# First layer, batch 0: routing logits after the projections, expert comparisons between copies, q and k scaled separately, experts in the last three steps

## The chip, the cores and the metric

The kernel runs on one core of a Trainium2 chip. The core has TensorE (PE in the profile; PEld is its weight load), VectorE (DVE), ScalarE (ACT), GpSimd (POOL) and SyncE (SP), each with its own in-order queue of instructions; semaphores order them. The metric is the device time of one execution, in microseconds (us).

## The reference, cut to what matters

Four layers run in a row over x of 8 x 512 tokens of 128 features. Layer 0, where nearly all of the change lies, is

```
xn = layernorm(x)
q, k, v = split(xn @ Wqkv)                     # 16 heads of 8
q, k = rms_norm(q, q_scale), rms_norm(k, k_scale)
attn = softmax(q k^T / sqrt(8)) v @ Wproj + bproj
logits = xn @ gate_w.T + gate_b                # 10 experts, the last 2 are empty
probs = softmax(logits); keep the top 2 of 10; renormalise over the true ones -> combine_w
ffn  = sum_e combine_w[:, e] * (xn @ expert_w[e] + expert_b[e])     # 8 true experts
x = x + attn + ffn
```

## The kernel before, in words

Layer 0 is two blocks. At the end of a block all engines meet, and only then does the next begin.

**layer0_norm** loads x and the weights and normalises x over 8 batches of 512 tokens. At its end, gate_logits (L264 to L274) multiplies each of the 32 tiles of 128 tokens by the 128x10 gate matrix, each fp32 product showing as two matmul records in the trace. When all are done, VectorE adds the gate's bias (L344), and the block ends.

**layer0_mix** is written out by hand, one queue per engine, over 8 batches of 16 steps. One step s handles 4 heads and 128 keys: TensorE computes `scores` in two halves (L708), ScalarE exponentiates each half (L494), and two steps later TensorE multiplies them with v (`times_v`, L722), four steps adding up in one bank. VectorE copies that bank out after each four (`copy_o`, L545), and the next group of four waits for that copy. Scores, projections, mean squares and the replicated q and k all go through a ring of three PSUM slots, whose order is the list ring_order0: a use waits until its slot's last user was read. So scores (0, 4) half 0 waits until `take_qk(1)` (L516) has read the projection of batch 1, which is issued in step 2.

Ahead of batch 0 come: `project` (q and k, L670), `project_v` (L677), VectorE's copies of them (L516, L522), GpSimd's squares (L462), `mean_square` (L684), ScalarE's `rms` chain of four activations over [128, 1024] (L473 to L479), `scale_qk` (L528 to L533: multiply, rounded high part, low part), `replicate` (L696) and `take_rep` (L538), which puts the copies into the stacks that scores reads. Two replicates, q and k of the first heads, stand ahead of step 0; the other two are issued in steps 0 and 1.

The routing of all tokens runs once, in batch 0: `route_start` (maximum and subtraction, L574, L576), ScalarE's exponential (L483), `route_probs` (L580 to L584), `precedence` (L303: 19 comparisons of each expert's probabilities with the others'), the rest of `route` (L590 to L605), TensorE's `turn_cw` (L755, two transposes into the bank ps_y), and VectorE's copy to cw_rows (L624). SP then stores that to DRAM and loads it back spread over all partitions (cwb, 2 MB, L452, and cwT, L453). `weigh` (L553) multiplies xn by one expert's weights, into three buffers in turn, and `expert` (L741) adds that expert's product up in ps_y. In batch 0 the experts are issued two a step in steps 12 to 15, in later batches one a step from step 8.

VectorE's queue ahead of and in batch 0 is, before: route_start, take_qk(0), take_v(0), route_probs, scale_qk(0), take_rep(0, 0), take_rep(0, 1), take_rep(0, 2), take_rep(0, 3), take_qk(1), precedence and route, wait for turn_cw, cw_rows, copy_o(0, 0), take_v(1), copy_o(0, 1), weigh 0 to 2, scale_qk(1), weigh 3, copy_o(0, 2), weigh 4 to 7, take_rep(1, 0), take_rep(1, 1). TensorE's turn_cw is issued in step 3.

## Time and profile before

| | |
|---|---|
| time, median of 3 runs (lowest to highest) | 1919.44 us (1919.16 to 1919.61) |
| the profiled execution's own time | 1919.56 us |
| its span | 1917.8 us |
| its mean granted TensorE clock | 0.95 |
| PE busy over the span | 1765.0 us (92%) |
| DVE, ACT, POOL busy | 53%, 44%, 17% |
| the mix block's batch 0 begins its scores at | 55.74 us |
| batch 1 begins its scores at | 121.24 us |
| batch 2 begins its scores at | 169.74 us |

The profile is of one execution. Its timeline lists instructions in order: start (us from the span's start), duration, engine and line, output<-inputs, shapes, count of a merged run, and in brackets the idle time before it and who ended that. A view of windows gives, for each stretch, the busy time of each engine and the granted TensorE clock, 1.00 being 2.4 GHz and 0.50 being 1.2 GHz.

### The profile page before, as it was taken

Reading aid. Unit: us, or ns where it says so; the run is one execution under the profiler, and the core shown is the slowest. Engines: PE = TensorE matmul, PEld = TensorE weight load, DVE = VectorE, ACT = ScalarE, POOL = GpSimd, SP = SyncE. Lnnn points to the kernel's source line nnn. Section 1 sums busy time; section 2 is a strip of 40 time slices with the busy share of each in tenths; the row PEclk is TensorE's granted clock in tenths of the full one; section 3 lists DMA queues with packets and bytes.
Section 4 is the critical chain, followed back from the end, with each engine's and each line's share of the span. In section 5 each row is a group of like instructions: output and inputs, shape, how many; then the busy total and the mean of one; then the engine's idle time right before and its main releaser. Section 6 shows DMA issues by size and latency. Waiting matters only on the chain. (4 is left out here: it accounts for less than half of the span.)

```text
span 1917.8 us, 23240 instructions
## 1 busy us (share of the span) xinstructions
PE 1765.0 (92%) x8678; PEld 1032.3 (54%) x8678; DVE 1014.4 (53%) x1676; ACT 845.4 (44%) x1025; POOL 329.3 (17%) x274
## 2 busy tenths in 40 slices
PE   6599999998887998999999999999999978999995
PEld 4222222222553445787878787878787824444442
DVE  3454545444675444544545454545445456777665
ACT  4467777785433333343434333333434243434341
POOL 1000000000463002112121212020303022232222
PEclk8689999998777999999999999999999989999998
DMA  1222222122002640000000000000000010000001
GB/s 72 41 51 45 45 45 45 45 45 115 1 1 71 157 126 1 1 1 1 1 2 1 1 1 1 1 1 1 1 1 1 1 52 1 0 0 0 0 0 44
DMA packets 19120, 48.95 MB, mean 26 GB/s; under 512 B 784, under 2 KB 1680, under 8 KB 18128
## 3 DMA queue, kind: packets, MB, share of 16 engines
q1 hardware_dynamic: 19024, 47.63, 10.2%
q8 instruction: 65, 1.06, 0.2%
q14 instruction: 31, 0.25, 0.0%
HBM read 45.14 MB, written 2.36 MB: 25 GB/s over the span
## 5 line engine op out<-in xcount | busy, mean ns | idle before, releaser
L494 ACT ACTIVATE probs<-ps_ring 128x1024 f32<-128x1024 f32 x256 | 246.1, 1024 | 126.6 <-PE ps_ring L708 123.9
L1765 PEld LDWEIGHTS ps_o<-v,probs 128*128 128x128 f32 x2048 | 235.3, 192 | 31.0 <-issue 25.6
L1765 PE MATMUL ps_o<-v,probs 128*128 128x129 f32 x2048 | 248.1, 278 | 1.7 <-ACT probs L1490 1.2
L1490 ACT ACTIVATE probs<-ps_ring 128x1024 f32<-128x1024 f32 x128 | 126.9, 1024 | 212.4 <-PE ps_ring L1746 212.3
L722 PE MATMUL ps_o<-probs,v 128*32 128x512 f32 x1024 | 140.1, 621 | 13.1 <-DVE o_sb L545 13.1
L1571 DVE TENSOR_REDUCE negmax<-ps_o 128x2 f32<-128x1024 f32 x64 | 78.5, 1226 | 137.2 <-PE ps_o L1721 137.2
L1958 POOL TENSOR_TENSOR rs<-r,state 128x512 f32<-128x512 f32 x64 | 81.6, 1275 | 206.3 <-DVE state L2050 202.6
L1483 ACT ACTIVATE xn<-ps_ring,pack 128x512 f32<-128x512 f32 x64 | 40.5, 685 | 162.6 <-PE ps_ring L1330 162.6
L708 PEld LDWEIGHTS ps_ring<-q_stack,k_stack 32*128 32x128 f32 x512 | 31.9, 188 | 123.2 <-issue 103.0
L1584 DVE RECIPROCAL rden<-ps_o 128x2 f32<-128x2 f32 x128 | 21.5, 168 | 144.1 <-PE ps_o L1765 144.1
L2050 DVE TENSOR_TENSOR_SCAN state<-decay,state,kv 128x511 f32<-128x511 f32 x64 | 91.5, 1430 | 5.9
L1330 PE MATMUL ps_ring<-gate_high,w_low 128*128 128x512 f32 x208 | 87.1, 419 | 2.0 <-DVEq L1547 1.6
L708 PE MATMUL ps_ring<-q_stack,k_stack 32*128 32x512 f32 x512 | 81.6, 517 | 5.2 <-ACT probs L494 2.9
L1571 DVE TENSOR_REDUCE negmax<-ps_ring 128x2 f32<-128x1024 f32 x64 | 75.4, 1221 | 15.1 <-PE ps_ring L1721 15.1
L1330 PE MATMUL ps_ring<-gate_high,w_high 128*128 128x512 f32 x208 | 82.1, 395 | 0.0
L1330 PE MATMUL ps_ring<-gate_low,w_high 128*128 128x512 f32 x208 | 81.8, 393 | 0.0
L1440 POOL TENSOR_TENSOR gate_low<-xn,gate_high 128x512 fp32r<-128x512 f32 x32 | 41.6, 1299 | 220.3 <-DVE gate_high L1564 220.3
L1208 DVE TENSOR_TENSOR hs<-h,score 128x512 f32<-128x512 f32 x64 | 44.0, 692 | 65.1 <-PE ps_y L1236 53.7
L741 PE MATMUL ps_y<-xe,pack 128*128 128x512 f32 x128 | 72.7, 656 | 4.6 <-DVE xe L553 4.6
L1330 PE MATMUL ps_ring<-xh,w_low 128*128 128x512 f32 x168 | 71.0, 423 | 4.6 <-POOL xl L1437 4.2
L545 DVE COPY o_sb<-ps_o 128x512 f32<-128x512 f32 x32 | 22.0, 688 | 97.7 <-PE ps_o L722 97.7
L1591 DVE SCALAR_TENSOR_TENSOR att<-ps_o,rden,att 128x128 f32<-128x128 f32 x224 | 68.4, 347 | 8.4
(371 smaller groups left out, 3473.6 us busy)
## 6 DMA issues: line engine op xcount, KB each, us to landing
cwb<-combine_by_expert SPq DMA_DIRECT2D x8, 2048.0 KB
score<-score_by_expert SPq DMA_DIRECT2D x7, 2048.0 KB, 13.8
pack<-pack_dram SPq DMA_DIRECT2D x1, 3840.0 KB, 15.8
pack<-pack_dram SPq DMA_DIRECT2D x1, 2443.0 KB, 8.6
x<-x_in SPq DMA_DIRECT2D x2, 1024.0 KB, 6.8
out<-x SPq DMA_DIRECT2D x1, 2048.0 KB, 6.3
score<-score_by_expert SPq DMA_DIRECT2D x1, 1536.0 KB, 13.3
pack<-pack_dram SPq DMA_DIRECT2D x1, 1451.0 KB, 7.1
```

The costliest lines, as they stand in the source:

```text
L494: nc.scalar.activation(probs[n % 3][:, 2 * half:2 * half + 2, :], ps, ACT.Exp, scale=float(HD0) ** -0.5).then_inc(read, 1)
L708: last = nc.tensor.matmul(ps[:, k, :], single(stacks["k"][b % 2][rows, g, m * P:(m + 1) * P]), single(stacks["q"][b % 2][rows, g, :]), sta ...
L722: last = nc.tensor.matmul(ps_o[32 * j:32 * j + 32, :], v[b % 2][:, m, 4 * g + j, :], probs[n % 3][:, j, :], start=(m == 0), stop=(m == NBL ...
L741: nc.tensor.matmul(ps_y[:, :], w["expert0"][:, e * P:(e + 1) * P], xe[:, n % 3, :], start=(e == 0), stop=False).then_inc(xe_used, 1)
L1208: nc.vector.tensor_tensor(hs[:, n % 3, :], h[:, n % HS1, :], score[b % 2][:, e, :], ALU.mult).then_inc(hs_ready, 1)
L1330: last = nc.tensor.matmul(out, single(lhsT), single(rhs), start=(start and n == 0), stop=(stop and n == 2))
L1490: nc.scalar.activation(probs[:, n % 2, m, :, :], ps, ACT.Exp).then_inc(read, 1)
L1571: nc.vector.reduce_max(negmax[:, n % 2, :, m], ps[:, :, :], AX_X, negate=True).then_inc(read, 1)
L1591: last = nc.vector.scalar_tensor_tensor(att[:, m, :], o[:, k, 0:D], rden[:, i, k:k + 1], att[:, m, :], ALU.mult, ALU.add)
L1765: last = nc.tensor.matmul(ps_o[:, i, k * (D + 1):(k + 1) * (D + 1)], probs[:, (b * PAIRS + p) % 2, m, j, queries], v[:, m, h, :], start=(m ...
L1958: nc.gpsimd.tensor_tensor(rs[:, j % 4, :], r[:, :], st[:, j, :], ALU.mult).then_inc(rs_ready, 1)
L2050: nc.vector.tensor_tensor_scan(st[:, j, 1:T], decay[:, 0:T - 1], kv[:, j % 2, 0:T - 1], st[:, j, 0:1], ALU.mult, ALU.add).then_inc(scanned, 1)
```

## The change

1. The gate's 32 tiles leave the norm block. Tiles 0 to 9 are issued after project_v(0) and tiles 10 to 31 after mean_square(0), both into ps_y. The bias addition becomes the first instruction of route_start.
2. For batch 0 the rms chain and the scaling run in halves: four activations over q, then four over k, and three VectorE instructions on each; replicate(0, 0) waits for the q half only. Later batches keep the whole-width forms, with semaphores counted in twos.
3. VectorE's queue becomes: take_qk(0), take_v(0), the two halves of scaling, take_rep(0, 0), take_rep(0, 1), route_start, take_rep(0, 2), route_probs, take_rep(0, 3), precedence, take_qk(1), the rest of route, copy_o(0, 0), take_v(1), the copy to cw_rows, copy_o(0, 1), scale_qk(1), weigh 0 to 2, copy_o(0, 2), weigh 3 and 4, take_rep(1, 0), weigh 5 to 7, take_rep(1, 1). ScalarE does the rms chain first, then waits for route_start and does the routing's exponential, then the scores.
4. turn_cw moves from step 3 to step 6. The experts of batch 0 move from steps 12 to 15 (2 each) to steps 13 (2), 14 (3) and 15 (3).
5. Layer 1 calls the new gate_logits in a loop over batches, with the same matmuls and waits as before.

```diff
@@ gate_logits
-    for t in range(NT):
-        if t % NBLK == 0:
-            pe.wait_ge(normed, t // NBLK + 1)
-        last = nc.tensor.matmul(ps[:, 0, t * n:(t + 1) * n], xn[:, t * P:(t + 1) * P], gate,
-                                start=True, stop=True)
-    last.then_inc(done, 1)
+    for t in tiles:
+        last = nc.tensor.matmul(ps[:, t * n:(t + 1) * n], xn[:, t * P:(t + 1) * P], gate, start=True, stop=True)
+    return last
@@ layer0_norm
-            gate_logits(nc, pe, xn, w["gate0"], ps, E0, normed, logits_done)
-            dve.wait_ge(logits_done, 1)
-            nc.vector.tensor_tensor(sh["logits0"][:, :, :], ps[:, 0, 0:NT * E0].rearrange("p (t e) -> p t e", e=E0),
-                                    w["gate0_b"].unsqueeze(1).broadcast_to([P, NT, E0]), ALU.add)
@@ layer0_mix, ScalarE
+            def first_rms(n):
+                ps, read = filled(act, ("ms", 0))
+                half = inv[:, n, :]
+                taken = nc.scalar.activation(half, ps[:, n, :], ACT.Ln, bias=bound[:, 8:9])
+                if n == 1:
+                    taken.then_inc(read, 1)
+                act.drain()
+                nc.scalar.activation(half, half, ACT.Exp, scale=0.5)
+                act.drain()
+                nc.scalar.activation(half, half, ACT.Ln, bias=bound[:, 9:10])
+                act.drain()
+                nc.scalar.activation(half, half, ACT.Exp, scale=-1.0).then_inc(inv_ready, 1)
...
+            act.wait_ge(bound_ready, 1)
+            first_rms(0)
+            first_rms(1)
             act.wait_ge(exp_in, 1)
             nc.scalar.activation(lg[:, :, :], lg[:, :, :], ACT.Exp).then_inc(exp_out, 1)
-            act.wait_ge(bound_ready, 1)
-            for step in range(4):
-                rms(0, step)
@@ layer0_mix, VectorE
+            def first_scale_qk(n, scale):
+                dve.wait_ge(inv_ready, n + 1)
+                last = nc.vector.scalar_tensor_tensor(qk[:, n, :], qk[:, n, :], w[scale], inv[:, n, :], ALU.mult, ALU.mult)
+                if n == 1:
+                    last.then_inc(scaled, 1)
+                dve.drain()
+                nc.vector.tensor_copy(single(high[:, n, :]), qk[:, n, :])
+                dve.drain()
+                nc.vector.tensor_tensor(single(low[:, n, :]), qk[:, n, :], high[:, n, :], ALU.subtract).then_inc(split_ready, 1)
...
             def route_start():
+                dve.wait_ge(logits_done, 1)
+                nc.vector.tensor_tensor(lg[:, :, :], ps_y[:, 0:NT * E0].rearrange("p (t e) -> p t e", e=E0),
+                                        w["gate0_b"].unsqueeze(1).broadcast_to([P, NT, E0]), ALU.add)
+                dve.drain()
...
-            route_start()
             take_qk(0)
             take_v(0)
-            route_probs()
-            scale_qk(0)
+            first_scale_qk(0, "qs_col")
+            first_scale_qk(1, "ks_col")
             take_rep(0, 0)
             take_rep(0, 1)
+            route_start()
             for b in range(B):
                 follows = b + 1 < B
                 take_rep(b, 2)
+                if b == 0:
+                    route_probs()
                 take_rep(b, 3)
+                if b == 0:
+                    precedence(nc, dve, lg, first, E0)
                 if follows:
                     take_qk(b + 1)
                 if b == 0:
                     route()
-                    dve.wait_ge(turned, 1)
-                    nc.vector.tensor_copy(cw_rows[:, :, :], ps_y[:, 0:2 * P].rearrange("p (k c) -> p k c", k=2)).then_inc(cw_ready, 1)
...
                 else:
+                    store_rows()
                     copy_o(b, 1)
+                if follows:
+                    scale_qk(b + 1)
+                if b == 0:
                     weigh(b, 0)
                     weigh(b, 1)
                     weigh(b, 2)
+                copy_o(b, 2)
+                for e in range(6 if b else 3, E0_TRUE):
+                    if b == 0 and e == 5:
+                        take_rep(b + 1, 0)
+                    weigh(b, e)
@@ layer0_mix, TensorE
-                pe.wait_ge(split_ready, b + 1)
+                pe.wait_ge(split_ready, 2 * b + 1 + n)
...
             project_v(0)
+            gate_logits(nc, xn, w["gate0"], ps_y, E0, range(0, 10))
             mean_square(0, 0)
             mean_square(0, 1)
+            gate_logits(nc, xn, w["gate0"], ps_y, E0, range(10, NT)).then_inc(logits_done, 1)
...
-                    if s == 3 and b == 0:
+                    if s == 6 and b == 0:
                         turn_cw()
...
-                    elif s >= 12:
-                        if s == 12:
+                    elif s >= 13:
+                        if s == 13:
                             pe.wait_ge(cw_ready, 1)
-                        expert(b, 2 * (s - 12))
-                        expert(b, 2 * (s - 12) + 1)
+                        for e in ((0, 1), (2, 3, 4), (5, 6, 7))[s - 13]:
+                            expert(b, e)
```

(store_rows holds the wait for turn_cw and the copy to cw_rows that stood behind route.)

## Rows read from the trace of the kernel before

**Rows 1.** Busy time by stretch: setup of the mix, batch 0, batch 1.

```profile
34.45:55.70 21.25, 9.28 (x24) 4.90 (x24) 12.13 (x21) 6.10 (x6) 4.99 (x5) 0.66 0.00 1
55.74:121.24 65.50, 50.23 (x229) 15.90 (x230) 29.98 (x49) 34.84 (x36) 2.07 (x1) 0.73 0.20 35
121.24:169.74 48.50, 45.31 (x264) 13.55 (x260) 23.74 (x28) 34.72 (x36) 1.89 (x1) 0.96 0.25 44
```

**Rows 2.** Timeline where the norm block ends: start, duration, engine, line.

```profile
27.14 0.69 DVE L246 TENSOR_TENSOR xn<-n_xc,xn 128x512 f32<-128x512 f32 x1 [0.58 <-ACT xn L259]
...
33.67 0.49 DVE L344 TENSOR_TENSOR logits<-n_ps,pack 128x320 f32<-128x320 f32 x1 [5.84 <-PE n_ps L272]
...
34.47 3.75 PE L670 MATMUL ps_ring<-xn,pack 128*128 128x512 f32 x4 [0.83 <-PEq L311]
```

**Rows 3.** One source line, the gate matmuls, before and after 29.1 us.

```profile
L272 PE MATMUL n_ps<-pack,xn x44: 174/258/341, 24.3 to 29.0; 128*128 128x10 f32 x44
...
L272 PE MATMUL n_ps<-pack,xn x22: 257/366/367, 28.9 to 33.3; 128*128 128x10 f32 x22
```

**Rows 4.** Timeline of the mix block, from its projections to the first scores.

```profile
38.26 1.22 DVE L516 COPY qk<-ps_ring 128x1024 f32<-128x1024 f32 x1 [0.16 <-PE ps_ring L670]
...
39.56 1.89 POOL L462 TENSOR_TENSOR sq<-qk 128x1024 f32<-128x1024 f32 x1 [2.01 <-DVE qk L516]
...
41.51 1.98 PE L684 MATMUL ps_ring<-sq,pack 128*128 128x512 f32 x4 [1.82 <-POOL sq L462]
...
43.59 1.11 ACT L473 ACTIVATE inv<-ps_ring,bound 128x1024 f32<-128x1024 f32 x1 [5.00 <-PE ps_ring L684]
...
47.13 1.06 ACT L479 ACTIVATE inv<-inv 128x1024 f32<-128x1024 f32 x1
...
48.22 1.41 DVE L528 SCALAR_TENSOR_TENSOR qk<-qk,pack,inv 128x512 f32<-128x512 f32 x2 [6.42 <-ACT inv L479]
...
50.49 1.22 DVE L533 TENSOR_TENSOR qk_low<-qk,qk_high 128x1024 fp32r<-128x1024 f32 x1
...
53.12 1.29 DVE L538 TENSOR_SCALAR q_stack<-ps_ring,bound 128x1024 fp32r<-128x1024 f32 x1 [1.41 <-PE ps_ring L696]
...
54.32 1.28 DVE L538 TENSOR_SCALAR k_stack<-ps_ring,bound 128x1024 fp32r<-128x1024 f32 x1
```

**Rows 5.** Groups by form, one activation of half the width.

```profile
L259 ACT ACTIVATE xn<-xn 128x512 f32<-128x512 f32 x2 | 1.3, 630 | 0.1
```

**Rows 6.** Busy time and granted clock, after the mean squares.

```profile
44.00:51.80 7.80, 0.00 (x0) 0.00 (x0) 3.33 (x4) 3.97 (x4) 0.00 (x0) 0.64 0.00 0
```

**Rows 7.** Timeline of the routing's exponential and the first scores.

```profile
38.12 0.47 ACT L483 ACTIVATE logits<-logits 128x320 f32<-128x320 f32 x1 [2.42 <-DVE logits L576]
...
56.57 3.85 ACT L494 ACTIVATE probs<-ps_ring 128x1024 f32<-128x1024 f32 x4 [8.39 <-PE ps_ring L708]
...
60.25 1.28 DVE L538 TENSOR_SCALAR k_stack<-ps_ring,bound 128x1024 fp32r<-128x1024 f32 x1 [1.53 <-PE ps_ring L696]
```

**Rows 8.** Timeline of batch 0, from the comparisons to batch 1.

```profile
66.55 6.47 DVE L303 TENSOR_TENSOR cwb<-logits 128x320 f32<-128x320 f32 x19
...
73.10 3.49 DVE L590 TENSOR_REDUCE rank<-cwb 128x320 f32<-128x3200 f32 x1
...
79.48 0.69 PE L755 MATMUL ps_y<-pack,cw 128*128 128x128 f32 x2 [12.07 <-DVE cw L605]
...
80.21 0.42 DVE L624 COPY cw_rows<-ps_y 128x256 f32<-128x256 f32 x1 [0.78 <-PE ps_y L755]
...
87.92 1.07 PE L722 MATMUL ps_o<-probs,v 128*32 128x512 f32 x8 [0.47 <-DVE o_sb L545]
...
98.39 1.90 DVE L553 TENSOR_TENSOR xe<-xn,cwb 128x512 f32<-128x512 f32 x3 [2.02 <-DMA cwT<-combine_by_expert]
...
103.96 3.76 PE L741 MATMUL ps_y<-xe,pack 128*128 128x512 f32 x4
...
121.24 0.50 PE L708 MATMUL ps_ring<-q_stack,k_stack 32*128 32x512 f32 x4
```

More of the change, by code:

```diff
@@ L264, in layer_norm, with gate_logits @@
     return tensor, vector, scalar, normed
-def gate_logits(nc, pe, xn, gate, ps, n, normed, done):
-    for t in range(NT):
-        if t % NBLK == 0:
-            pe.wait_ge(normed, t // NBLK + 1)
-        last = nc.tensor.matmul(ps[:, 0, t * n:(t + 1) * n], xn[:, t * P:(t + 1) * P], gate,
-                                start=True, stop=True)
-    last.then_inc(done, 1)
+def gate_logits(nc, xn, gate, ps, n, tiles):
+    for t in tiles:
+        last = nc.tensor.matmul(ps[:, t * n:(t + 1) * n], xn[:, t * P:(t + 1) * P], gate, start=True, stop=True)
+    return last
 def over(a, n):
@@ L417, in layer0_mix @@
         cw_loaded, biased = sem("cw_loaded"), sem("biased")
-        exp_in, exp_out, combined, turned, cw_ready, cw_stored = (
-            sem(n) for n in ("exp_in", "exp_out", "combined", "turned", "cw_rows_ready", "cw_stored"))
+        logits_done, exp_in, exp_out, combined, turned, cw_ready, cw_stored = (
+            sem(n) for n in ("logits_done", "exp_in", "exp_out", "combined", "turned", "cw_rows_ready", "cw_stored"))
         block = ctx.enter_context(nc.Block())
@@ L478, in rms @@
                 else:
[L479 removed]
+                    nc.scalar.activation(inv[:, :, :], inv[:, :, :], ACT.Exp, scale=-1.0).then_inc(inv_ready, 2)
                 act.drain()
+            act.wait_ge(bound_ready, 1)
+            first_rms(0)
+            first_rms(1)
             act.wait_ge(exp_in, 1)
             nc.scalar.activation(lg[:, :, :], lg[:, :, :], ACT.Exp).then_inc(exp_out, 1)
[L484 to L486 removed]
             for b in range(B):
@@ L532, in scale_qk @@
                 dve.drain()
-                nc.vector.tensor_tensor(single(low[:, :, :]), qk[:, :, :], high[:, :, :], ALU.subtract).then_inc(split_ready, 1)
+                nc.vector.tensor_tensor(single(low[:, :, :]), qk[:, :, :], high[:, :, :], ALU.subtract).then_inc(split_ready, 2)
             def take_rep(b, i):
@@ L587, in route @@
             def route():
-                precedence(nc, dve, lg, first, E0)
                 nc.vector.reduce_sum(rank[:, :, :], first[:, :, :, :], AX_X)
@@ L646, in _ @@
                     weigh(b, 2)
-                if follows:
-                    scale_qk(b + 1)
-                if b == 0:
-                    weigh(b, 3)
-                copy_o(b, 2)
-                for e in range(6 if b else 4, E0_TRUE):
-                    weigh(b, e)
-                if follows:
-                    take_rep(b + 1, 0)
+                copy_o(b, 2)
[3 more added lines that the diff above has]
+                    weigh(b, e)
+                if b and follows:
+                    take_rep(b + 1, 0)
+                if follows:
                     take_rep(b + 1, 1)
@@ L962, in _ @@
             pe.wait_ge(sh["w_loaded"][1], 16)
-            gate_logits(nc, pe, xn, w["gate1"], ps, E1, normed, logits_done)
+            for b in range(B):
+                pe.wait_ge(normed, b + 1)
+                last = gate_logits(nc, xn, w["gate1"], ps[:, BANK_LOGITS, :], E1, range(b * NBLK, (b + 1) * NBLK))
+            last.then_inc(logits_done, 1)
             for b in range(B + 1):
```

12 lines of the change are left out of this document (6 added, 6 removed).

## The prediction

> **What bounds the kernel now.** I read the busy shares and the 40 slices of the page first. PE is busy most of the span, so only a stretch where PE waits for one chain can give much. Then the windows: batch 1 takes 48.50 us from its first scores to the next batch's, and PE is busy 45.31 of them. Batch 0 takes 65.50 us with PE busy 50.23, so PE stands idle 15.3 us, and its granted clock is 0.73 against 0.96 in batch 1 [rows 1]. Ahead of batch 0 lie 21.25 us with PE busy 9.28. All that the change touches lies in these two stretches. From batch 1 on every queue is the same as before, and each transfer is issued behind an event of its own batch, so what is won before batch 1's scores should arrive at the end in full. So I work out two things: how much earlier the first scores come (55.74), and how much shorter the way from there to batch 1's scores (121.24) gets.
>
> The timeline shows the causes. The gate's records keep PE until about 33.6 [rows 3], and VectorE's addition ends at 33.67 + 0.49 = 34.16; the norm's last own instruction ended at 27.14 + 0.69 = 27.83. The mix begins 0.3 us after the block's end [rows 2]. In batch 0 PE waits 12.07 us for the routing (at 79.48), and ACT, starved by it, too [rows 8].
>
> **Part 1: to the first scores.** I call R the end of take_rep(0, 1): before, 54.32 + 1.28 = 55.60 [rows 4].
>
> The block ends 34.16 - 27.83 = 6.33 us earlier, so PE's projections start at 34.47 - 6.33 = 28.14 [rows 2]. They took 3.75 us for four records at 1.2 GHz; the mean squares took 1.98 for four of the same size at 2.4 [rows 2, 4]. The clock was at 1.00 until 29.0 before. I take two records at each level, 0.9 us less; the bounds are 0 and 1.8. The copy of q and k goes from 38.26 to 38.26 - 6.33 - 0.9 = 31.0, and the squares, 1.89 us behind it, end at 34.2 instead of 41.45 [rows 4].
>
> Now PE has the first 10 gate tiles in front of the mean squares. The rate: 44 records in 4.75 us up to 29.0, that is 0.108 us each; 22 in 4.4 us after, 0.207 each, the first at 2.4 GHz and the second at 1.2 [rows 3]. Ten tiles are 20 records: 2.2 or 4.1 us. project_v ends near 32.5, so the mean squares start at 34.8 (36.6 at the lower clock) rather than at 34.2: the move costs 0.6 us here (bounds 0 and 2.4). ScalarE starts 2.08 us after them, as before (43.59 - 41.51), at 36.9.
>
> Its chain was 43.59 to 47.13 + 1.06 = 48.19, 4.60 us for four activations 1024 wide [rows 4]. Half as wide, one takes 0.63 to 0.67 [rows 5], with a 0.07 gap 0.72: 2.88 a half and 5.75 for both, 1.15 more in all. But VectorE begins on q when half is through, and what is left behind the k half is short. The whole scaling took 48.22 to 51.71, 3.49 us: 1.41 + 1.22 + 0.86 for the rounding and gaps [rows 4]. A half is 0.70 + 0.69 (the 512-wide DVE instruction [rows 2]) + 0.57 = 1.96. From there before, two replicates and two copies took until 55.60, 3.89 us; now the q copy follows the k scaling at once while PE replicates k, whose copy can start 1.41 us after its split (VectorE's wait for a replicate before) and takes 1.28: 2.7 in all [rows 4]. R = 36.9 + 5.75 + 1.96 + 2.7 = 47.3, if the gate's other 22 tiles are out of PE's way. They are 44 records, 4.75 us or 9.1 us: PE gets to replicate(0, 0) at 41.6 or 45.9. The first hides behind the scaling; the second gives R = 45.9 + 3.89 = 49.8. With the clock falling midway PE is free near 44, R = 47.9. I take R = 47.7, a gain of 7.9 us (bounds 5.6 and 8.8).
>
> A rule speaks against this part. After PE's last record the clock stayed at 1.00 for over 2 us and then fell: mean 0.64 over 7.8 us of idleness [rows 6]. The Trainium skill, "TensorE: Matmul & The Clock Gate", section "HAM oscillation — how this bites in real kernels", says that a TensorE which waits between bursts falls back to half rate and starts the next burst slow. The gate's matmuls filled 24.3 to 28.1, and PE is now idle there; by the rule all of the projections would run at the lower level and R would be 48.6 instead. That loss of 0.9 us is within the bounds above, which come from the rows alone.
>
> **Part 2: from R to batch 1's scores.** I follow the queues, in us after R.
>
> VectorE: route_start is three instructions 320 wide at 0.49 [rows 2] with gaps, done at 1.65. ScalarE then takes 0.47 for the exponential [rows 7] and begins the scores at 2.2; before it began them at 56.57 - 55.60 = 0.97. This new wait is the change's main cost, 1.2 us: the whole first steps are queued behind it on ScalarE, PE waits for their ring slots, and take_rep(0, 3), which came at 60.25 - 55.60 = 4.65, now comes at 5.9 and ends at 7.2 [rows 7]. take_rep(0, 2) and route_probs (under 1.6 us) fit in front, in time in which VectorE waits for PE. precedence is 6.47 [rows 8], to 13.75; take_qk(1) 1.22, to 15.0; the rest of route 73.10 to 79.42 (turn_cw began at 79.48), 6.32, to 21.35 [rows 4, 8]. Before it ended at 79.42 - 55.60 = 23.8. So the routing ends 2.5 us sooner after R, because take_qk no longer waits for a projection at 1.2 GHz in front of it: the projection (from 7.2, 3.8 us) now runs beside the comparisons.
>
> PE: with turn_cw gone from step 3 it does step 3 and two times_v, then waits for the ring slot of take_qk(1) until 15.0, and then steps 4, 5, 6 run beside the rest of route. Two scores and a times_v, with 1.94 us of ScalarE per step (3.85 for four halves) [rows 7], bring PE to turn_cw at 21.4 to 22.6. The 12 us stall shrinks to some 1 to 2 us. copy_o(0, 0) and take_v(1) are 0.69 each, so the copy to cw_rows ends near 23.5; before at 80.21 + 0.42 - 55.60 = 25.0. times_v(4) starts at 22.7, before at 87.92 - 55.60 = 32.3: here the attention work is 9.6 us ahead.
>
> The transfer: from cw_rows' end (80.63) to the first weigh (98.39) are 17.76 us [rows 8]. Nothing in the change shortens that: the first weigh comes at 41.3 and the first expert at 42.0. PE meanwhile needed 103.96 - 87.92 = 16.0 us from times_v(4) to step 12's experts, and has times_v(10) and step 13's scores (1.4) to do besides: it stands at the experts at 40.2. So the transfer is what is late next, and the 9.6 us ahead become 103.96 - 55.60 = 48.4 less 42.0, 6.4 us. From the first expert to batch 1's scores before: 121.24 - 103.96 = 17.28, now less 1.43 for times_v(10) and step 13's scores, which are already done, and less 0.5 for a wait on xe in step 14: 15.35. VectorE keeps up: weigh 0 to 4 are done before PE asks, weigh 5 to 7 at 0.65 each follow take_rep(1, 0), each behind an expert 1 us long. Batch 1's scores: 42.0 + 15.4 = 57.4 after R, before 121.24 - 55.60 = 65.64. Gain 8.2 us. Bounds: experts 0 and 1 took 3.76 for four records, at 1.2 GHz, against 1.98 for four of this size at 2.4 [rows 4, 8]; with that clock up already it is 10.0; with route and the start of PE's steps 1.5 us later and VectorE's buffers once in the way, 5.7. As a test from the other side: PE's idle time in batch 0 would go from 15.3 to about 7 us, so the gain can't pass 15.3 - even at the same clock [rows 1].
>
> **The sum.** 7.9 + 8.2 = 16.1. From the profiled execution's own 1919.56 (span 1917.8): 1903.5; that execution is 0.1 above the median 1919.44, so 1903.3.
>
> **The rivals.**
> A (likeliest, 0.66): as worked out, 1903.3; its own range 1900.5 to 1907.
> B (0.17): PE's clock falls in the gate's second share and stays low. The 22 tiles then hold replicate(0, 0): R at 49.8 to 50.5, and steps 4 to 6 run at 1.2 GHz, so turn_cw is 1 us later. Gain 5.4 + 7.0: 1907.0. For it: before, the clock fell under just these matmuls [rows 3]. Against: 20 of them are ahead of the mean squares now, and these run at full width.
> C (0.10): batch 0 gains nothing, since the transfer and VectorE's longer queue between 41 and 52 us after R (five weighs, two take_reps, a copy_o) hold the experts, three a step, until the old time. Only part 1 is left: 1911.5. Against it: it needs 8 us more on VectorE, whose queue there is 8 x 0.65 + 2 x 1.28 + 0.69 = 8.5 us long and starts as soon as the data lands.
> D (0.04): the gain is given back by a later stage and nothing changes: 1919.4. Nothing I see from batch 1 on waits for a fixed time.
> E (0.03), the other side: the wait for take_qk(1) behind the comparisons leaves PE so thinly busy that the clock stays at 1.2 GHz through all of batch 0. A times_v of 1.07 would take about double, and with the scores' part a step costs some 1.2 us more (an estimate from the doubled record times); 8 experts, 16 records at 0.94 against 0.50, cost 7 [rows 4, 8]: 16 x 1.2 + 7 = 26 us on a PE that was at 0.73 already, which had paid about half; about 19 more, less 16.1: 1922. It decides from about 32 us of extra PE work at the lower level, each costing half.
>
> **How the numbers follow.** 0.2% is 3.8 us, about what a measurement tells from no change. A, B and C are faster (0.93), D is the same (0.04), E slower (0.03). The range 1900 to 1909 takes in A's bounds and B (0.83) and leaves out C's rest, D and E; its low end is 7.9 + 10.0 + 1.
>
> **What would show it.** Right: projections at 28.1; ACT's first Ln near 36.9; first scores at 47.5 to 48.5; turn_cw with under 2 us of wait in front; the 12 us stall gone; the first weigh waiting for cwT about 41 us after R; batch 1's scores at 105.1; batch 1 itself still 48.5. Wrong: replicate(0, 0) waiting behind gate matmuls with the clock at 0.5 (B); weighs that wait for xe_used, or experts for xe, by more than 1 us (C); a batch 1 longer than 49 (D); a clock under 0.6 over all of batch 0 (E). The estimate I trust least is the 5.75 + 1.96 of the halves beside the clock of the gate's 44 records.

## The result

The four times on record are 1894.76, 1895.37, 1900.12 and 1900.52 us, median 1897.74; the kernel before, in the same four rounds, 1919.3 (1918.43 to 1919.61). The ratio is 0.9893, 95% interval 0.9873 to 0.9913: faster by 1.1%. I had forecast 1903.3 with a range from 1900 to 1909. The direction and the kind of gain came as forecast, the median lies 5.6 us below it and 2.3 below the range.

The page of the changed kernel, profiled in the execution of 1894.76 us:

```profile
span 1893.0 us, 23251 instructions
...
PE 1760.1 (93%) x8678; PEld 1030.3 (54%) x8678; DVE 1012.6 (53%) x1678; ACT 846.2 (45%) x1029; POOL 329.3 (17%) x274
```

Its busy time by stretch, from the mix's start to the end of take_rep(0, 1), from there to batch 1's scores, and batch 1 (columns: stretch, length, busy time of PE, PEld, DVE, ACT, POOL with counts, granted clock, DMA share, GB/s):

```profile
27.48:46.50 19.02, 17.58 (x88) 13.57 (x88) 10.48 (x19) 6.51 (x9) 5.02 (x5) 0.70 0.00 1
46.50:101.24 54.74, 50.04 (x228) 16.19 (x229) 30.52 (x56) 35.04 (x37) 1.90 (x1) 0.76 0.25 42
101.24:149.67 48.43, 45.26 (x264) 13.47 (x260) 23.74 (x28) 34.72 (x36) 1.89 (x1) 0.96 0.27 44
```

PE's idle time from R, the end of take_rep(0, 1), to batch 1's scores is 54.74 - 50.04 = 4.7 us; in batch 0 of [rows 1] it was 15.3. Batch 1 is as long as it was. The timeline of the changed kernel, up to the comparisons (line numbers have moved: L696 projections, L270 gate, L710 mean squares, L463 first Ln, L531 scaling, L552 take_rep, L498 scores' exponential, L300 comparisons, L520 take_qk, L607 the rest of route):

```profile
27.52 2.99 PE L696 MATMUL ps_ring<-xn,pack 128*128 128x512 f32 x4 [3.69 <-PEq L308]
...
31.88 2.30 PE L270 MATMUL ps_y<-pack,xn 128*128 128x10 f32 x20
...
34.03 1.96 PE L710 MATMUL ps_ring<-sq,pack 128*128 128x512 f32 x4
...
35.83 6.91 PE L270 MATMUL ps_y<-pack,xn 128*128 128x10 f32 x44
...
36.09 0.69 ACT L463 ACTIVATE inv<-ps_ring,bound 128x512 f32<-128x512 f32 x1 [7.33 <-PE ps_ring L710]
...
39.00 0.75 DVE L531 SCALAR_TENSOR_TENSOR qk<-qk,pack,inv 128x512 f32<-128x512 f32 x1 [6.23 <-ACT inv L471]
...
45.22 1.28 DVE L552 TENSOR_SCALAR k_stack<-ps_ring,bound 128x1024 fp32r<-128x1024 f32 x1
...
48.43 5.75 ACT L498 ACTIVATE probs<-ps_ring 128x1024 f32<-128x1024 f32 x6
...
52.10 1.28 DVE L552 TENSOR_SCALAR k_stack<-ps_ring,bound 128x1024 fp32r<-128x1024 f32 x1 [1.08 <-PE ps_ring L722]
...
53.30 4.77 DVE L300 TENSOR_TENSOR cwb<-logits 128x320 f32<-128x320 f32 x19
...
58.15 1.23 DVE L520 COPY qk<-ps_ring 128x1024 f32<-128x1024 f32 x1
...
59.29 3.48 DVE L607 TENSOR_REDUCE rank<-cwb 128x320 f32<-128x3200 f32 x1
```

And on to batch 1 (L781 turn_cw, L627 cw_rows, L567 weigh, L767 expert, L734 scores):

```profile
65.95 0.44 PE L781 MATMUL ps_y<-pack,cw 128*128 128x128 f32 x2
...
66.86 0.42 DVE L627 COPY cw_rows<-ps_y 128x256 f32<-128x256 f32 x1
...
85.42 1.89 DVE L567 TENSOR_TENSOR xe<-xn,cwb 128x512 f32<-128x512 f32 x3 [1.28 <-DMA cwT<-combine_by_expert]
...
86.26 3.69 PE L767 MATMUL ps_y<-xe,pack 128*128 128x512 f32 x4 [1.05 <-DVE xe L567]
...
101.24 0.50 PE L734 MATMUL ps_ring<-q_stack,k_stack 32*128 32x512 f32 x4
```

The reader is to see three things. The 12.07 us wait in front of turn_cw [rows 8] is gone. The 19 comparisons take 4.77 us where they took 6.47 [rows 8]. And PE waits 1.05 us for the first expert's input, which waited for the transfer.

I compare kernels by five marks, all read from such rows. The mark of batch 1 is the moment at which SP issues batch 1's weights (120.40 before), 0.84 us ahead of its scores; the end is SP's issue of the output.

| profiled execution of | mix starts | to R | R to weights out | to first weigh | batch 1's mark | mark to end |
|---|---|---|---|---|---|---|
| before | 34.42 | 21.18 | 25.06 | 17.73 | 120.40 | 1790.66 |
| changed, on record | 27.48 | 19.02 | 20.81 | 18.11 | 100.40 | 1785.88 |
| my forecast | 28.1 | 19.6 | 23.5 | 17.8 | 104.3 | 1790.7 |

The end comes 24.8 us earlier: 20.0 of them are won by batch 1's mark and 4.8 behind it, where the matmuls and waits are as before. That pair of numbers is what the experiments had to explain.

### The profile page after: what moved, and what is told of

It is laid out like the page before. It is cut to its first block and busy times, and to the rows that moved or that the text cites. A ratio compares the mean times of both kernels' runs of the same rounds, so it can differ in the third digit from the quotient of the medians.

```text
span 1893.0 us, 23251 instructions
## 1 busy us (share of the span) xinstructions
PE 1760.1 (93%) x8678; PEld 1030.3 (54%) x8678; DVE 1012.6 (53%) x1678; ACT 846.2 (45%) x1029; POOL 329.3 (17%) x274
## 5 line engine op out<-in xcount | busy, mean ns | idle before, releaser
L498 ACT ACTIVATE probs<-ps_ring 128x1024 f32<-128x1024 f32 x256 | 245.9, 1024 | 104.8 <-PE ps_ring L734 101.8
L734 PEld LDWEIGHTS ps_ring<-q_stack,k_stack 32*128 32x128 f32 x512 | 32.2, 188 | 125.7 <-issue 103.3
L734 PE MATMUL ps_ring<-q_stack,k_stack 32*128 32x512 f32 x512 | 82.3, 515 | 5.7 <-ACT probs L498 3.6
L767 PE MATMUL ps_y<-xe,pack 128*128 128x512 f32 x128 | 72.4, 655 | 5.1 <-DVE xe L567 5.1
L1225 ACT ACTIVATE h<-ps_h 128x512 f32<-128x512 f32 x64 | 38.2, 597 | 75.7 <-PE ps_h L1262 75.7
```

What stands on the lines that cost most here:

```text
L498: nc.scalar.activation(probs[n % 3][:, 2 * half:2 * half + 2, :], ps, ACT.Exp, scale=float(HD0) ** -0.5).then_inc(read, 1)
L734: last = nc.tensor.matmul(ps[:, k, :], single(stacks["k"][b % 2][rows, g, m * P:(m + 1) * P]), single(stacks["q"][b % 2][rows, g, :]), sta ...
L767: nc.tensor.matmul(ps_y[:, :], w["expert0"][:, e * P:(e + 1) * P], xe[:, n % 3, :], start=(e == 0), stop=False).then_inc(xe_used, 1)
```

## The experiments

Sixteen runs were made, each beside the kernel before: ten altered kernels, two of them twice, and the two kernels of the change unaltered again. A table of their marks stands behind the first group.

**The same two kernels again.** No edit.

> The changed kernel, unaltered. Its four times were 1894.8, 1895.4, 1900.1 and 1900.5 us, two pairs 5 us apart; the one profile is of 1894.8, and there batch 1's scores come 20.0 us earlier than before the change and the end 24.8 us earlier. Theory: the 20.0 us of batch 0 are the same in every execution, and the rest comes from where the stretches of lower TensorE clock fall in later work, which differs between executions; then this run's landmark at batch 1 is again 101.2 us (within 0.8), while the time is anywhere from 1894 to 1901. Rival: the two kinds of execution differ in batch 0 itself; then the landmark moves by about 5 us with the time.

> The changed kernel, unaltered, a third profile. Theory: from the mix's start to batch 1 between 72.9 and 76 us, comparisons 4.8 us, and the distance from there to the end anywhere between 1784 and 1791, with a time that follows from the two. Rival, by the first profile: the change shortens the distance to the end by 4.8 us as well; then it is near 1786.

> The changed kernel, unaltered, a fourth profile. Theory: batch 1 reached 17 to 20 us earlier than before, 37.5 to 40.6 us after take_rep(0, 1) for the first weigh, and a median over the six times of 1900 to 1903, with single times from 1894 to 1907. Rival: the first four times are the kernel's and the later ones a slower chip's; then the median here is below 1898 again or the kernel before moves with it.

> The kernel before, unaltered, for a second profile. Theory: how the stretches of lower TensorE clock fall differs between executions and is worth up to 5 us, in batch 0 (up to 3 us) and behind it; then the distance from batch 1's scores to the end, 1790.7 us in the first profile of this kernel and 1785.9 and 1790.3 in the two of the changed one, lies anywhere between 1784 and 1791 here. Rival: that distance belongs to the kernel; then it is 1790.7 within 0.5 again.

| profiled execution of | to R | R to weights out | batch 1's mark | mark to end | times, median (lowest to highest) |
|---|---|---|---|---|---|
| again_1 | 19.72 | 20.80 | 103.72 | 1790.30 | 1902.2 (1894.5 to 1906.2), 6 |
| again_2 | 21.12 | 20.68 | 101.78 | 1793.16 | 1902.8 (1897.8 to 1906.8), 7 |
| again_3 | 19.69 | 20.81 | 103.97 | 1790.38 | 1899.9 (1894.6 to 1903.9), 6 |
| before_again | 21.18 | 25.07 | 120.79 | 1789.82 | 1919.1, 1 |
| before_sq_held | 22.57 | 22.97 | 118.89 | 1790.38 | 1918.1 (1912.0 to 1921.8), 10 |
| qk_first | 22.98 | 26.34 | 108.82 | 1784.41 | 1899.2 (1898.4 to 1901.7), 4 |
| qk_first_2 | 23.04 | 26.33 | 108.73 | 1784.37 | 1900.3 (1897.8 to 1902.9), 5 |
| qk_first_squares_held | 19.14 | 24.63 | 106.79 | 1786.05 | 1900.2 (1897.0 to 1901.7), 4 |
| turn_step3 | 21.15 | 28.41 | 109.26 | 1785.81 | 1906.9 (1903.5 to 1909.1), 4 |
| part_1_only | 19.14 | 27.22 | 116.36 | 1786.22 | 1916.4 (1911.1 to 1919.9), 10 |
| experts_from_12 | 19.78 | 20.82 | 105.19 | 1785.94 | 1900.8 (1897.9 to 1907.4), 5 |
| whole_width | 22.39 | 20.86 | 105.86 | 1790.59 | 1902.5 (1897.7 to 1907.4), 4 |
| load_in_halves | 19.02 | 20.80 | 97.81 | 1788.07 | 1895.5 (1894.1 to 1897.4), 4 |
| halves_2 | 21.12 | 20.67 | 99.52 | 1788.57 | 1896.6 (1894.1 to 1897.1), 5 |
| halves_from_12 | 19.74 | 20.81 | 101.10 | 1786.30 | 1898.1 (1896.0 to 1899.8), 4 |
| scores_first | 21.12 | 19.93 | 99.28 | 1788.88 | 1895.2 (1893.2 to 1896.6), 4 |

The mark moved between 100.40 and 103.97 for one and the same kernel, so my theory that batch 0's 20.0 us are fixed fell; its rival, that the mark follows the time, doesn't hold alone either (again_2 has the mark at 101.78 and a time of 1903.4). The distance to the end moved too, between 1785.88 and 1793.16, further than I had written. Over all runs the changed kernel has 23 times from 1894.5 to 1906.8 with median 1901.4, the kernel before 58 from 1912.7 to 1926.9 with median 1918.2: a difference of 16.8 us. The second profile of the kernel before has 1789.8 for the distance, 0.8 below its first and so outside the 0.5 of the rival; the other kernels' distances, with the same code behind the mark, speak against it too. On again_3's chip the changed kernel has a median of 1899.9 and the kernel before 1918.2, so a slower chip behind the later times is not seen.

Where does it come from? In two kernels that have batch 1 word for word alike, the windows from mark to mark, and of the next block (layer 1's routing and attention). Of qk_first:

```profile
108.82:155.70 46.88, 43.71 (x264) 13.31 (x260) 23.74 (x28) 34.72 (x36) 1.89 (x1) 1.00 0.27 46
448.54:588.32 139.78, 113.93 (x522) 65.62 (x522) 92.14 (x231) 57.29 (x108) 71.88 (x64) 0.76 0.10 41
```

Of again_2:

```profile
101.78:150.22 48.44, 45.26 (x264) 13.56 (x260) 23.74 (x28) 34.72 (x36) 1.89 (x1) 0.96 0.26 44
444.64:589.70 145.06, 120.96 (x522) 70.46 (x522) 92.38 (x231) 57.30 (x109) 71.87 (x64) 0.71 0.10 40
```

The same instructions: DVE, ACT and POOL are busy the same time to 0.3 us, and only PE's time and the granted clock differ. A batch takes 46.88 us at 1.00 and 48.44 at 0.96; the layer-1 block 139.78 at 0.76 and 145.06 at 0.71. Between mark and end the two profiles differ by 8.8 us: 3.1 in batches 1 to 6 (284.70 against 287.82), 5.3 in the layer-1 block, 0.3 in the rest.

It is not all chance. Batch 1 took 46.87 to 46.90 us in seven of the eighteen profiles and 48.43 to 48.51 in the other eleven, and the profiles of one kernel always fall on one side: both of the kernel before and all four of the changed one took the long form, both of qk_first and both of load_in_halves the short one. In all eighteen PE waits 2.0 us for VectorE's copy_o, until some 10 us behind the mark. Four microseconds from 1.0 us before that wait's end, in the changed kernel and in qk_first:

```profile
109.20:113.20 4.00, 3.03 (x16) 0.72 (x20) 0.82 (x2) 0.27 (x1) 1.89 (x1) 0.63 1.01 156
117.60:121.60 4.00, 3.01 (x28) 0.92 (x32) 0.84 (x2) 1.41 (x2) 1.89 (x1) 1.00 1.03 168
```

In the long form the granted clock falls to 0.50 for about 3 us there, in the short one it stays at 1.00. Batches 2 to 6 take either form too, and the profiles of one kernel can differ in them. Over all eighteen profiles the six batches together took 284.7 to 287.9 us, the layer-1 block 136.5 to 145.1, all that follows 1304.6 to 1306.0. What decides which form a batch takes, no run here shows.

**The comparisons and GpSimd's squares.**

```diff
# qk_first, qk_first_2
-                if b == 0:
-                    precedence(nc, dve, lg, first, E0)
                 if follows:
                     take_qk(b + 1)
+                if b == 0:
+                    precedence(nc, dve, lg, first, E0)
# qk_first_squares_held: that, and; before_sq_held: this alone, in the kernel before
                 was_read(pool, ("qk", b))
+                if b == 1:
+                    pool.wait_ge(combined, 1)
```

> The changed kernel with take_qk(1) put back in front of the comparisons. Theory: the copy waits for a projection that ends near 57.2 us, GpSimd's squares of batch 1 then run beside the comparisons and hold one of them for their whole 1.9 us, as before the change; comparisons 6.5 us instead of 4.8, the routing ends 5.7 us later (1.7 of it the hold, 4.0 the wait for the projection), and since the transfer of the weights decides when the experts start, batch 1's scores come 5.7 us later: about +5.7 us. Rival: TensorE's steps, not the routing, set the pace, and the order of the two costs under 2 us.

> As the run before, but GpSimd's squares of batch 1 wait until the routing's weights are ready, so that they no longer run beside the comparisons. Theory of the held port: the comparisons take 4.8 us again, and the time is 1.7 us below the run before, +4.0 over the changed kernel. Rival: the comparisons were slow before the change for another reason (their memory, ScalarE beside them); then they take 6.5 us here too, and nothing is won.

> The kernel before with one wait added: GpSimd's squares of batch 1 wait for the routing's end. Nothing else. Theory of the held port: the 19 comparisons take 4.8 us instead of 6.47, the routing ends 1.7 us earlier, the squares are still in time for step 7, and batch 1's scores come 1.7 us earlier, beside up to 1.5 us either way from the clock. Rival: the comparisons stay at 6.5 us and nothing moves.

> take_qk(1) in front of the comparisons again, a second profile of it. In the first, batch 0 took 81.4 us from the mix's start to batch 1 against 72.9 and 75.9 in the two of the changed kernel, but the distance to the end was 1784.4, the shortest seen, and the times (1898.4 to 1901.7) are level with the changed kernel's. Theory: chance placement of the clock; this profile has batch 0 near 79 to 80 and over these times together the order costs 3 to 6 us. Rival: what batch 0 loses here is always given back behind it; then the distance to the end is 1784 to 1785 again.

One source line of the kernel before, its comparisons (durations in ns: least, median, greatest):

```profile
L303 DVE TENSOR_TENSOR cwb<-logits x19: 205/344/1908, 66.5 to 72.8; 128x32 f32<-128x32 f32 x2, 128x288 f32<-128x288 f32 x2, 128x64 f32<-128x64 f32 x2, 128x256 f32<-128x256 f32 x2
```

The groups by form in the same stretch, of the two 128x32 comparisons and of GpSimd's squares (busy us, mean ns, idle before):

```profile
L303 DVE TENSOR_TENSOR cwb<-logits 128x32 f32<-128x32 f32 x2 | 2.1, 1056 | 0.0
...
L462 POOL TENSOR_TENSOR sq<-qk 128x1024 f32<-128x1024 f32 x1 | 2.1, 2071 | 25.3 <-DVE qk L516 25.3
```

The same line in the changed kernel:

```profile
L300 DVE TENSOR_TENSOR cwb<-logits x19: 208/319/484, 53.3 to 57.9; 128x32 f32<-128x32 f32 x2, 128x288 f32<-128x288 f32 x2, 128x64 f32<-128x64 f32 x2, 128x256 f32<-128x256 f32 x2
```

One comparison of 32 elements took 1908 ns, its twin 205: 1.7 us, the whole difference between 6.47 and 4.77. With take_qk(1) put in front again (qk_first, timeline), the squares run beside the comparisons and these take 6.48; with the squares held as well, 4.77, and the weights leave 24.63 after R instead of 26.34. (The expected 1.7 us don't show in its time, 1900.2 against 1899.2; its first weigh came 21.0 us after the weights left, where qk_first has 18.3.) And in the kernel before, with that wait alone:

```profile
66.78 4.77 DVE L303 TENSOR_TENSOR cwb<-logits 128x320 f32<-128x320 f32 x19
...
78.11 1.89 POOL L464 TENSOR_TENSOR sq<-qk 128x1024 f32<-128x1024 f32 x1 [37.43 <-DVE cw L607]
```

So the held instruction is shown in both directions. In part_1_only, where route_probs stands behind take_qk(1), the hold falls on its multiplication instead, 1.43 us where such an instruction takes 0.49, while the reciprocal ahead of it, with one input, takes its usual 0.35 beside the same squares:

```profile
58.58 0.35 DVE L600 RECIPROCAL stat<-stat 128x32 f32<-128x32 f32 x1
59.01 1.43 DVE L602 TENSOR_TENSOR logits<-logits,stat 128x320 f32<-128x320 f32 x1
...
58.19 1.89 POOL L454 TENSOR_TENSOR sq<-qk 128x1024 f32<-128x1024 f32 x1 [24.72 <-DVE qk L520]
```

The Trainium skill, "SBUF — State Buffer", section "Who interferes with whom", says that VectorE and GpSimd share one pair of ports, which is locked for a whole instruction, and that a VectorE instruction with two SBUF inputs needs it against a GpSimd instruction that reads SBUF. The trace agrees in each of these rows: the held instructions have two inputs in SBUF, and the one in part_1_only ends 0.36 us after the squares do (60.44 and 60.08).

The effect on the whole is another matter. The order cost batch 0 what I had said and more (marks 108.8 and 108.7 against 100.4 to 104.0), but both profiles have the shortest distance to the end of all, 1784.4, and the nine times (median 1899.7) are level with the changed kernel's. For the times my theory fell, and the rival of the second run held: what batch 0 loses is given back behind it. The first run's rival had the times right, under 2 us, but not its reason, since the mark did move. before_sq_held reached batch 1 1.5 and 1.9 us earlier than the two profiles of the kernel before, and its times show nothing: ratio 1.0000 (0.9978 to 1.0021).

**turn_cw back in step 3.**

```diff
-                    if s == 6 and b == 0:
+                    if s == 3 and b == 0:
                         turn_cw()
```

> The changed kernel with turn_cw put back to step 3. Theory: TensorE stands before the routing's end (65.6 us) with three steps of attention still to do; from turn_cw to the first expert it needed 24.5 us before the change, so the first expert comes near 90.5 instead of 86.2: +4.3 us. Rival: the transfer of the weights bounds the experts in any case, and the move is worth under 1 us.

The median is 5.5 us above the changed kernel's 1901.4. The timeline:

```profile
67.02 0.69 PE L781 MATMUL ps_y<-pack,cw 128*128 128x128 f32 x2 [7.45 <-DVE cw L622]
```

PE stands waiting again, for 7.45 us. The cost reached further than I had reckoned: VectorE has copy_o(0, 0) ahead of the copy to cw_rows, and that needs the attention steps that PE now does behind turn_cw, so the weights leave 28.41 after R instead of 20.8, and the mark moves by 5.3 to 8.9 us instead of 4.3.

**The other parts.** In part_1_only the gate and the halves stay and all of part 2 is undone, but for scale_qk(1), which stands ahead of the weighs, and take_rep(1, 0), which stands ahead of weigh 5, both as in the changed kernel; route_start stays behind take_rep(0, 1), because it needs the moved gate:

```diff
                 take_rep(b, 2)
-                if b == 0:
-                    route_probs()
                 take_rep(b, 3)
-                if b == 0:
-                    precedence(nc, dve, lg, first, E0)
                 if follows:
                     take_qk(b + 1)
                 if b == 0:
+                    route_probs()
+                    precedence(nc, dve, lg, first, E0)
                     route()
+                    store_rows()
# and turn_cw in step 3; with experts_from_12:
+                    weigh(b, 3)
                 copy_o(b, 2)
...
+                    elif s >= 12:
+                        if s == 12:
+                            pe.wait_ge(cw_ready, 1)
+                        expert(b, 2 * (s - 12))
+                        expert(b, 2 * (s - 12) + 1)
# whole_width
-            first_rms(0)
-            first_rms(1)
+            for step in range(4):
+                rms(0, step)
...
-            first_scale_qk(0, "qs_col")
-            first_scale_qk(1, "ks_col")
+            scale_qk(0)
```

> The moved gate and the halves alone: VectorE's order in batch 0, turn_cw in step 3 and the experts from step 12 are as before the change (route_probs directly ahead of the comparisons, the copy to cw_rows directly behind the routing). Theory: scores can start 19 to 21 us after the mix's start, at 46.5 to 48 as in the changed kernel; ScalarE's wait for the routing's start makes take_rep(0, 3) 1.2 us later, route_probs adds 1.5, and the rest is as before, so the weights go out 27.8 us after take_rep(0, 1) (25.1 before, 20.8 in the changed kernel) and batch 1 is reached near 114.8 against 120.4 before and 100.4 to 103.7 in the changed kernel: part 1 is worth about 6 us on its own, part 2 the other 12. Rival: most of the gain is the shorter norm block and start; then this kernel reaches batch 1 within 3 us of the changed one.

> The changed kernel with the experts of batch 0 back in steps 12 to 15, two a step (and weigh 3 ahead of the copy of the third group, without which this order can't run). Theory: the transfer sets when the first expert runs, and a whole step more of attention then stands behind it: 16.4 us from the first expert to batch 1's mark before, 14.1 in the changed kernel, so +2.3 us. Rival: TensorE reaches the experts after the data in either case, and nothing changes.

> The changed kernel with q and k scaled in one chain 1024 wide again. Theory: ScalarE 4.6 and VectorE 3.5 us in line and then two replicates and copies, 12.0 us from the first Ln to the end of take_rep(0, 1), against 10.4 in the changed kernel: scores and batch 1 1.6 us later, if the gate's last tiles hide behind the chain. Rival: with the clock low the gate's tiles hold the replicates in both, and the halves win nothing (under 0.5).

part_1_only reaches batch 1 at 116.36, 1.6 later than expected, and 4.0 to 4.4 earlier than before; its ratio is 0.9989 (0.9974 to 1.0005). The first weigh there came 24.8 us after the weights left, behind scale_qk(1), not behind the transfer, so this kernel is not quite part 1 alone. PE stood waiting 2.27 us for that weigh; about so much the old order of the two could give back (an estimate from that wait, not run). Most of the gain, some 12 to 16 us at batch 1's mark less these 2.3, needs part 2. experts_from_12 waits 3.92 us for the first expert instead of 1.05 to 2.37 and reaches batch 1 at 105.19, 1.2 to 4.8 later than the changed kernel (2.3 expected). whole_width takes 12.00 us from the first Ln to R. Of the fifteen profiles with the moved gate fourteen have halves: twelve of them take 10.39 to 10.53, so the 1.6 us came as expected; the two of qk_first take 12.76, because there the gate's last tiles hold the replicate (shown below), which is the rival. Batch 1 comes at 105.86, R after 22.39. In the times both (1900.8, 1902.5) can't be told from the changed kernel.

**A better version.** The weights of batch 0 loaded as two transfers:

```diff
# load_in_halves, halves_2
+                if b == 0:
+                    for h in range(2):
+                        sp.dma_start(cwb[:, 4 * h:4 * h + 4, :], here[4 * h:4 * h + 4].unsqueeze(0).broadcast_to([P, 4, T])
+                                     ).then_inc(cw_half[h], 16)
...
+                if b == 0 and e % 4 == 0:
+                    dve.wait_ge(cw_half[e // 4], 17)
# halves_from_12: also weigh 0 to 2 ahead of scale_qk(1), experts from step 12 as above
# scores_first: load_in_halves, and in ScalarE's loop, behind step 0's two exponentials
+                    if n == 0:
+                        act.wait_ge(exp_in, 1)
+                        nc.scalar.activation(lg[:, :, :], lg[:, :, :], ACT.Exp).then_inc(exp_out, 1)
```

(cw_half are two semaphores that already stood at 1. With this edit weigh 0 also no longer waits for cwT, which is loaded behind the 2 MB; what the split and what that gives was not separated.)

> The changed kernel with batch 0's 2 MB of weights loaded as two transfers of 4 experts each, weigh 0 waiting for the first alone. Theory: weigh 0 starts behind scale_qk(1) at once, 1.2 us earlier, and TensorE loses its wait of 1.0 us for the first expert: -1.0 us, no more, because TensorE gets there only then. Rival: the transfer's tail is what holds the last experts; then -3 us or more.

> load_in_halves again, for a second profile and more times. Its first four were 1894.1 to 1897.4 and batch 1 came at 97.8 us, 2.6 to 5.9 earlier than in three profiles of the changed kernel, where I had expected 1.0. Theory: the transfer's wait held TensorE idle at the lower clock, so the first two experts ran in 3.7 us instead of 2.6 as well; here batch 1 again comes at 97.5 to 99.5 and the median is 3 to 6 us below that of the changed kernel. Rival: placement of the clock by luck; then the medians are within 1.5 us.

> load_in_halves with weigh 0 to 2 ahead of scale_qk(1) and the experts from step 12, two a step. Theory: with the first half of the weights there near 78 us, experts 0 and 1 fit into a step in which TensorE waits for ScalarE; 1 to 2 us below load_in_halves. Rival: TensorE is the limit from step 11 on and the order is worth nothing, or scale_qk(1) comes later and replicate(1, 0) waits for it (+1 us).

> load_in_halves with ScalarE's exponential of the routing moved behind the two exponentials of step 0. Theory: ScalarE's first scores start 1.2 us earlier and take_rep(0, 3) too, while the probabilities come 1.9 us later, so the comparisons begin at the same time and batch 1 is reached within 0.5 us of load_in_halves. Rival by my prediction, which called that wait the change's main cost: 1.2 us are won.

The timeline of load_in_halves at the first expert (L575 weigh, L775 expert):

```profile
83.72 1.89 DVE L575 TENSOR_TENSOR xe<-xn,cwb 128x512 f32<-128x512 f32 x3
...
84.80 2.55 PE L775 MATMUL ps_y<-xe,pack 128*128 128x512 f32 x4
```

PE no longer waits, and its first two experts take 2.55 us (3.06 in halves_2) instead of 3.69: the clock rose while they ran (mean 0.60 from 80.5 to 87.3 us, against 0.51 from 82.5 to 89.9 in the changed kernel). The first weigh comes 16.8 and 16.6 us after the weights left, not 18.0 to 19.4, and the mark 14.1 and 14.6 us behind it, not 15.0 to 16.0: more than the 1.0 us I expected. The rival's cause doesn't show, for the changed kernel's PE doesn't wait for the last experts either. Over nine times the median is 1896.6 (1894.1 to 1897.4), beside 1901.4 over 23 for the changed kernel; with both on one chip, 1896.6 against 1899.9. It is the fastest version that was measured twice, 1.2% below the kernel before (ratio 0.9883, 0.9867 to 0.9899). halves_from_12 is later than it at the mark (101.10) and its times (median 1898.1) are no lower: its theory fell. Its weigh 0 waited 4.64 us for the first half, which came at 80.76 and not near 78, 12.3 us after the weights left, and PE then waited twice for xe (0.52 and 0.67). scores_first has mark 99.28 and median 1895.2; that is level with halves_2 in the profile, and the times don't settle the last microsecond.

## Why the prediction was wrong

The mechanism was as forecast; one term was mis-sized, and the range left out a spread that the kernel has. The profiled execution ended 8.7 us earlier than the sum: 2.7 from the way from R to the weights' leaving, 4.8 behind batch 1, 1.2 from the other terms. By its own terms, from the profile on record and the table above:

- **The shorter norm block**, 6.33 us: 6.94 in the profile on record, of which 0.6 is that the norm itself ended earlier. The mix's start lies between 26.56 and 28.23 in the fifteen profiled executions with the shorter norm block, and between 33.65 and 36.73 before. Right.
- **From the mix's start to R**, 19.6: 19.02, 19.72, 21.12 and 19.69. The ten gate tiles took 2.30 (2.2 forecast), the mean squares started at 34.03 (34.8), ScalarE at 36.09 (36.9). The halves gave what I had worked out, two times 2.9 us for ScalarE and 2.0 for VectorE's last half. Rival B's mechanism exists: in qk_first, whose code is the same up to here, the gate's matmuls reached right up to the replicate, at a clock of 0.50:

```profile
43.79 2.93 PE L270 MATMUL ps_y<-pack,xn 128*128 128x10 f32 x13
46.65 0.79 PE L722 MATMUL ps_ring<-qk_high,sel 32*128 32x512 f32 x2
```

and R came 23 us after the start. Both profiles of qk_first have it, none of the other thirteen with the moved gate. The order of take_qk(1) can't be the cause, since it stands behind; what is, the runs don't tell.
- **From R to the weights' leaving**, 23.5 forecast, 20.8 measured in every profile of the changed kernel. This is the step that failed: 2.7 us too much in part 2 of the sum. I took the 6.47 us of the comparisons from [rows 8] as the price of 19 instructions. 1.7 us of it was one instruction held by GpSimd's squares, and the new order takes the squares out of its way, because they wait for take_qk(1). The list of durations of that line, with its maximum of 1908 ns beside a median of 344, would have shown it. The other 1.0 us is small change: take_rep(0, 3) ended 6.9 after R instead of 7.2, the copies behind it ran closer together, and turn_cw found PE ready at once (65.95, 0.34 after the routing's end) where I had allowed up to 1 us.
- **The transfer**, 17.76: 18.0 to 19.4, so it gave back 0.2 to 1.7 of those 2.7 us. That it would be what is late next was right: PE waits 1.05 to 2.37 us behind it, and load_in_halves, which takes it away, is worth 3 to 5 us.
- **From the first weigh to batch 1's mark**, 15.3 forecast: 14.98 in the profile on record, 15.4 to 16.0 in the other three. Over the four profiles of the changed kernel the mark is at 102.5 on average, 1.8 us before the forecast: the 2.7 us less what the other terms took back. VectorE kept up; rival C can be struck.
- **Behind batch 1**, 0 forecast: 4.8 in the profile on record, 0.3 to 0.4 in again_1 and again_3, -2.5 in again_2. Of the 4.8, batches 1 to 6 are 1.7, the layer-1 block 2.3, the rest 0.8. On average the 0 was right (1789.9 over four profiles, 1790.2 over the two before). That was the second failure, and the larger: not a term of the sum, but the width of the range. I had reckoned with three times of the kernel before within 0.5 us and taken the distance to the end as fixed. Over many runs both kernels spread by more than 12 us, with the clock. That the result on record lies below the range is in part luck: its four times happened to hold two of the lowest four of 23. The 23 have their median at 1901.4, 1.9 us below the forecast, and 16 lie between 1900 and 1909. The gain between the medians of all runs, 16.8 us, is 0.7 above the sum's 16.1, and 1.3 less than the 18.1 that the marks give on average (120.6 before, 102.5 changed); that difference is below what these runs tell.

The wait that part 2 called the change's main cost, 1.2 us of ScalarE's for the routing's start, cost little: scores_first takes it away, and its weights leave 0.7 us sooner after R than in halves_2, its mark comes 0.4 us sooner. In rival E the working doesn't close: half of 26 us is 13, which less 16.1 would still be faster than before; batch 0 ran at 0.76 and nothing hung on it. Part 1's lower bound, 5.6, is 5.8 by its own numbers (55.6 - 49.8).

The projections, at a clock that fell while they ran, took 2.99 us in the profile on record, as in my sum (3.75 - 0.9 = 2.85), and 3.61 in again_2; in again_1 and again_3 they ran at 0.50 from end to end and took 3.75. PE had stood 3.69 us in front of them in the first. The rule that I cited from the Trainium skill, "TensorE: Matmul & The Clock Gate", section "HAM oscillation — how this bites in real kernels", that a TensorE which waits between bursts starts the next one slow, so fits two of four profiles in full, for 0.8 us; in the one on record the burst began at 1.00 and fell to 0.50 within its first microsecond.

What stays open: why qk_first loses 4.8 to 8.4 us by batch 1's mark and has the shortest distances behind it in both of its profiles. Of the 1.5 to 8.8 us by which that distance is below the changed kernel's, 1.5 to 3.2 are in batches 1 to 6, batch 1 in its short form among them, and 0.3 to 5.3 in the layer-1 block. Its two profiles agree to 0.1 us in each of these stretches; why it falls on the good side, the runs don't tell.

## What to carry to other kernels

A group's total is not its instruction count times a price: look at the greatest duration beside the median, and at what GpSimd did in that moment, before a total is carried to a new place in the order. When a long wait is taken out of a starved stretch, ask which transfer was hidden behind it and split that one too; here that gave another 3 to 5 us. Three times that agree to 0.02% say nothing of how a kernel's times spread with the clock (12 us here): a profile shows by how much a stretch differs at 0.96 and at 1.00, and the range has to hold that difference for each such stretch.

## What the runs showed of the hardware

A VectorE instruction with two inputs in SBUF waited for the whole of a GpSimd multiplication (32 elements in 1.9 us instead of 0.2; 320 in 1.43 instead of 0.49), one with a single input ran on beside it (0.35), and so did the 3.48 us reduction of the changed kernel beside the squares of 1.90 (3.49 in the kernel before, without them beside it). The same batch of 264 PE records took 46.88 us at a granted clock of 1.00 and 48.44 at 0.96; for batch 1, all profiles of one kernel agree on which. Of two transfers of 1 MB issued one behind the other the first was there 12.3 us after the weights left (halves_from_12); one transfer of 2 MB, with 16 KB behind it, let its first reader start after 18.0 to 19.4. Under the 44 records of gate matmuls 10 columns wide, issued back to back with PE shown busy throughout, the granted clock fell from 1.00 to 0.50 (at 38.5 us in the profile on record). Executions of one unaltered kernel differed by 12.3 us (1894.5 to 1906.8) with spans that follow their times and mean clocks between 0.949 and 0.958.
